# A graph attention kernel: ScalarE's node copies moved to the end of its round

## The reference, cut to what matters

```
xh = (h @ W).reshape(n, heads, d)
a_s = (xh * att_src).sum(-1)
a_d = (xh * att_dst).sum(-1)
alpha = leaky_relu(a_s[src] + a_d[dst], 0.2)
e = exp(alpha - amax[dst])
z = segment_sum(e, dst)
out = segment_sum(xh[src] * (e / z[dst])[:, :, None], dst)
```

## Time and profile before

| | |
|---|---|
| median of three runs | 9329.89 us (9316.76 to 9336.9) |
| the profiled execution's own time | 9341.26 us |
| its span | 9339.6 us |
| TensorE (matmul) busy | 5257.9 us, 56% |
| VectorE busy | 5523.9 us, 59% |
| ScalarE busy | 1794.4 us, 19% |
| GpSimd busy | 5226.3 us, 56% |
| edge stage of layer 0, first gather to last fade | 253.0 to 2840.6 us |
| edge stage of layer 1 | 3044.7 to 5649.0 us |
| edge stage of layer 2 | 5864.5 to 8462.8 us |

### The profile page before, as it was taken

How to read it: one execution, slowest core, us unless ns; L and a number is a source line. 1 busy time by engine, 2 the same in 40 slices (tenths; PEclk the granted TensorE clock), 3 DMA queues, 4 the chain that set the end, 5 groups by cost and what they waited for, 6 DMA issues and landing times. The chain is left out here.

```text
span 9339.6 us, 122620 instructions
## 1 busy us (share of the span) xinstructions
PE 5257.9 (56%) x21872; PEld 3686.3 (39%) x21873; DVE 5523.9 (59%) x14694; ACT 1794.4 (19%) x6145; POOL 5226.3 (56%) x5539
## 2 busy tenths in 40 slices
PE   4256565555556255555655556266666655553497
PEld 2144444433334144444433334144444443333255
DVE  4356565655558366666665658356666666558543
ACT  2011111110103022222210102122222221012333
POOL 3566666666662566666666662566666666661332
PEclk7577777776767577777776766677777777666699
DMA  3344444444442344444443333344444443334333
GB/s 119 115 141 134 140 136 138 141 133 135 135 132 87 110 117 119 117 118 119 118 118 112 110 113 109 109 118 127 123 123 122 125 123 111 111 112 136 106 54 76
DMA packets 541784, 1107.22 MB, mean 119 GB/s; under 512 B 125282, under 2 KB 333647, under 8 KB 541155
## 3 DMA queue, kind: packets, MB, share of 16 engines
q0 software_dynamic: 274368, 731.65, 29.1%
q1 hardware_dynamic: 265811, 370.32, 12.2%
q10 hardware_dynamic: 1152, 1.05, 0.0%
HBM read 962.72 MB, written 148.65 MB: 119 GB/s over the span
## 5 line engine op out<-in xcount | busy, mean ns | idle before, releaser
L1126 POOL DMA_INDIRECT edges_G<-rows,edges_index x4980 | 4767.6, 957 | 2943.5 <-issue 1374.7
L1320 PE MATMUL edges_ps_o<-edges_G,edges_OH 128*128 128x264 f32 x9960 | 3617.4, 516 | 2804.4 <-DVE acc L1584 1660.1
L1320 PEld LDWEIGHTS edges_ps_o<-edges_G,edges_OH 128*128 128x128 f32 x9960 | 2347.7, 252 | 3769.9 <-DVE acc L1584 1761.1
L1584 DVE TENSOR_TENSOR acc<-acc,edges_ps_o 128x264 f32 x2490 | 1057.2, 425 | 1934.0 <-remote 897.5
L1566 DVE TENSOR_TENSOR edges_G<-edges_G,edges_ps_c 128x1024 f32<-128x1024 f32 x1245 | 1501.5, 1206 | 56.6 <-ACT edges_G L1154 48.8
L1145 ACT ACTIVATE edges_node<-terms 128x12 bf16 x2490 | 494.5, 210 | 2463.1 <-issue 2432.5
L1558 DVE TENSOR_TENSOR edges_OH<-edges_ps_c,relT 128x512 f32<-128x512 f32 x1245 | 847.4, 681 | 37.5 <-issue 25.0
L1153 ACT ACTIVATE edges_ps_c<-edges_diff 128x80 f32<-128x80 f32 x249 | 60.0, 241 | 2316.3 <-DVE edges_diff L1546 2153.2
L2403 POOL DMA_INDIRECT x<-experts_Y,experts_token x105 | 162.1, 1544 | 373.1 <-issue 213.5
L1479 DVE TENSOR_TENSOR_SCAN edges_run<-edges_masks,edges_ps_s 128x128 f32<-128x128 bf16 x249 | 102.9, 413 | 424.1 <-ACT edges_fade L1163 256.4
L1278 PEld LDWEIGHTS edges_ps_s<-edges_node,edges_OHT 128*128 128x128 bf16 x4980 | 180.4, 103 | 209.0 <-issue 178.9
(11 more groups left out here) (345 smaller groups left out, 6340.4 us busy)
## 6 DMA issues: line engine op xcount, KB each, us to landing
edges_rels<-rel SPq DMA_DIRECT2D x249, 640.0 KB
edges_G<-rows,edges_index POOLq DMA_INDIRECT x4980
xslot<-edges_blank SPq DMA_DIRECT2D x80, 650.0 KB
edges_masks<-lanes SPq DMA_DIRECT2D x249, 96.0 KB
rows<-node_ext POOLq DMA_DIRECT2D x147, 130.0 KB, 2.4
experts_X<-xslot SPq DMA_DIRECT2D x105, 130.0 KB, 2.1
node_rows<-rows SPq DMA_DIRECT2D x98, 130.0 KB, 2.1
edges_xm<-xn SPq DMA_DIRECT2D x98, 128.0 KB
```

Of the source, the lines that this page charges most:

```text
L1126: g.indirect_dma_start(G[n][:, s, 0:RW], None, dr["rows"], bass.IndirectOffsetOnAxis(index[n][:, s:s + 1], 0)).then_inc(gathered[n], 16)
L1320: mm = pe.matmul(ps_o[BANK_OF[g]][:, 0:GW], OH[:, 2 * g + j, :], G[n][:, 2 * g + j, :], start=(j == 0), stop=(j == 1))
L1584: v.tensor_tensor(a, a, ps_o[BANK_OF[g]][:, 0:GW], ALU.add).then_inc(added, 1)
```

## The change

In ScalarE's round the call of `load_node` moves behind `fades` and `mixes`. No operation, operand or wait changes.

```
                 if exists(i, n, 1):
                     exponentials(*later(i, n, 1))
-                if exists(i, n) and exists(i, n, RING):
-                    load_node(i + 1, n)
                 if exists(i, n, 1):
                     fades(*later(i, n, 1))
                 if mix:
                     mixes(i, n)
+                if exists(i, n) and exists(i, n, RING):
+                    load_node(i + 1, n)
```

## The result

The changed kernel takes 9316.04 us (median of 20 runs, 9305.33 to 9321.03), the kernel before 9329.95 us beside it (20 runs, 9316.76 to 9342.34). The ratio is 0.9985, 95% interval 0.9978 to 0.9992: 14 us less, where 70 us were forecast. That lies within the 0.2% that the prediction took as no change. The profiled execution took 9317.66 us for a span of 9316.1 us, 23.5 us less than the one of before.

A forecast was written before the change was run, and what follows sets the result against it. The prediction took something that comes with the gathers and slows all engines to hold the rounds. The median 9329.9 us less 70 us, a sixth of the scan's 424 us wait, gave 9260 us; range 9130 to 9400 us.

The forecast's parts named there:

- a sixth of 424 us, 70 us: VectorE's idle time ahead of the scan: the share whose removal would shorten the whole run, between nothing and 256 us.
- the slope of 0.2: Layer 0's two groups of rounds: each 1 us of idle time ahead of the scan lengthens a round 0.2 us.
- Rival 1: Edge rounds: the gathers' cadence holds the round, so VectorE's wait only moves to the additions; 9330 us, chance 20%.
- the 256: VectorE ahead of the scan: 256 us of wait named as the fade's, taken as what leaves VectorE.
- under 150: Sign of being right: idle time ahead of the scan (L1479) falls from 424 us to under 150 us.
- ended by the turn: Sign of being right: what is left of the scan's idle time is ended by TensorE's turn (L1287).
- Costing ScalarE's later end at nothing: ScalarE's copies moved last: delay to centring and exponentials costed at nothing, with 127 us kept as the end.
- rival 3: ScalarE comes late to the next round's centring and exponentials, VectorE waits; 9394 us, at the far end 9457; chance 15%.
- rivals 3 and 4: Slower cases: ScalarE late to the next round (15%); copies colliding with TensorE's spread, 62 us, 9392 us (5%).
- cover of some 10 us: TensorE's spread (L1278) comes 10 us or more after the moved copies end; beyond that, every microsecond would stop TensorE.
- Rival 2: VectorE's wait for the fade is fully on the path, saving 256 us; 9074 us, chance 9%.
- Rival 5: ScalarE's node copies weren't what held the fade, so the change removes nothing; chance 3%.

The follow-up runs named there:

- double_again: The changed kernel with seven more node copies a round into a tile nobody reads; 9373.63 us, 0.9999 of the kernel before, at the upper level.
- static_before: The kernel before with constant block numbers in the node copies, so no register instructions between them; 7851.08 us, 0.9999 of the kernel before.
- double_after: The changed kernel with seven more node copies a round into a tile nobody reads; 7853.47 us, 1.0002 of the kernel before, at the lower level.

## Why the prediction was right or wrong

**The failed step: "a sixth of 424 us, 70 us", the part of the scan's wait that reaches the end.** The mechanism that leads up to it held (the fade came earlier and the scan's wait went), and this term was too large. Three measurements at the upper level give 0.9985, 0.9996 and 0.9991, by their medians 13.9, 6.7 and 11.5 us, so a fortieth of 424 us. I took the slope of 0.2 from two groups of eight rounds in layer 0, against the two stretches of layer 1, which showed none. In the 40 rounds of layer 2 above, the scan's wait grew by 38 us while a round got 0.1 us shorter. The two groups of layer 0 were 0.4 us a round apart, and in the trace of the kernel before, 24 groups of eight rounds (from the ninth round of each layer on) lie between 30.1 and 31.5 us a round: such a pair shows how rounds scatter, not a slope.

**Rival 1 is what the runs fit,** with its forecast of 9330 us and its sign in the profile: time left L1479 and time came ahead of L1584, 266.5 and 187.1 us in one profile, 231.1 and 183.3 in another. I had given it 20%, although the 30.7 us a round in the earlier trace rows "whether VectorE waits for the fade or not" was its whole case. What is shown for it: with the gathers left out, and the copies in their old place, the scan never waits, the additions wait 244 us in all, and the order gains nothing; and with the gathers in, copies made quick leave the rounds as long as they were. What is not shown is the path by which late instructions set the round at the upper level. It isn't GpSimd's issue alone, since GpSimd pauses for 1518.5 us there.

**What was right.** The scan's wait fell, by 266.5 us, where I had counted on 256. That the two are so near is in part luck: the 256 were the wait named as the fade's, of which 214.1 went, and the rest came from waits of other names that I had left out; the second pair of profiles gives 231.1. The fade comes 5 to 9 us after the exponentials in six rounds of ten. GpSimd's pauses fell "a little", by 16 us. Three signs were missed: the scan's idle time is 157.6 us, where under 150 was said; a round was to be 0.3 us shorter and is 14 / 249 = 0.06 us shorter; and what is left of the scan's wait was to be ended by the turn, where the largest part, 60.7 us, is "issue".

**Costing ScalarE's later end at nothing held.** The idle time ahead of L1243 fell from 559.5 us in layer 1 (551.6 for the 48 of the earlier trace rows) and 603.4 in layer 2 to 416.3 and 372.2, as rival 3 has it, but it did not run out, and the exponentials still waited 1232.3 us for their differences. TensorE's spread didn't wait longer either, the kernel before and then the changed one:

```profile
L1278 PE MATMUL edges_ps_s<-edges_node,edges_OHT 128*128 128x12 bf16 x4980 | 172.7, 172 | 134.2 <-DVE edges_run L1479 64.2 <-issue 52.3 <-DVE edges_OHT L1452 17.7
```
```profile
L1278 PE MATMUL edges_ps_s<-edges_node,edges_OHT 128*128 128x12 bf16 x4980 | 172.7, 172 | 133.7 <-issue 72.5 <-DVE edges_run L1479 61.2
```

So rivals 3 and 4 (copies late, or in the spread's way) don't show. How much of the cover of some 10 us ahead of the spread is needed, no run tells; `double_again` used 1.2 us more of it.

**Rival 2,** the wait fully on the path, would have been 9074 us, and no run came near.

**Rival 5** needed quick copies. In the changed kernel the register instructions between them still take from 2 to 1658 ns (whole trace):

```profile
L1145 ACTq ALU_OP  x4731: 2/38/1658, 249.3 to 8384.9; - x198
```

and in the one without gathers:

```profile
L1142 ACTq ALU_OP  x4731: 35/38/43, 249.8 to 5811.1; - x198
```

The Trainium skill ("Runtime: NRT & Kernel Launch", section Instruction fetch mechanics) has it that fetching is hidden, because the sequencer dispatches slower than its store of instructions is filled. By that all ten copies would go like the first four, in 2.4 us, and the change would gain nothing. Without gathers the trace agrees, with 2.4 us, and also at the lower level the register instructions are even; at the upper level with gathers they are not. Whether it is fetching that is late there, no run shows.

## What to carry to other kernels

A wait that looks as if it lay on the path is worth only what a round gets shorter without it. Compare many rounds with and without the wait before taking a slope from two groups, and ask first how far such groups scatter. If gaps appear on all engines with nothing waited for, ask first what they share. One run that leaves the shared suspect out (here the gathers: 9244 to 6744 us) told more here than the reordering did. Count what an edit adds before reading it: seven copies that share their neighbours' addresses were not seven slow copies. And run the unchanged kernel in every batch, since its own level can move by more than the change under study.

## What was not expected of the hardware

- One and the same kernel ran at 7851 to 7854 us in three batches and at 9244 to 9377 us in four measurements, nearly all runs of a batch within 0.4% of each other, and on a chip of the same number at both. The lower level was traced only in edited kernels (such as `static_before` and `double_after`), not in the kernel before or the changed one themselves.
- At the upper level register instructions of ScalarE and VectorE take up to 1.7 us instead of 0.04, and additions wait 1160.2 us for sums under "remote", as if these were seen late. With half of the gathers the time is 6899 us, against 6744 without any, and the longest such instruction between ScalarE's copies takes 0.7 us.
- An indirect gather of 128 rows takes GpSimd 0.95 us and 0.3 us of issue whether it moves 260 words a row or 16, and one of 260 words lands 2.6 us after the end of its issue when it is alone.
